# The selective scan of a fused four-layer kernel: VectorE's product of a state with its C rows is issued one recurrence later

## The reference

```python
dt = jax.nn.softplus(ts @ W_dt.T + b_dt)      # b, L, 1024
A = -jnp.exp(A_log)                           # 1024, 16

def step(state, inp):                         # state: b, 1024, 16
    dt_t, B_t, C_t, u_t = inp
    dA = jnp.exp(dt_t[..., None] * A)
    state = state * dA + (dt_t * u_t)[..., None] * B_t[:, None, :]
    y = jnp.einsum('bdn,bn->bd', state, C_t)
    return (state, y)
_, ys = jax.lax.scan(step, init, xs)
y = ys.transpose(1, 0, 2) + x * D
y = y * jax.nn.silu(gate)
return y @ W_out.T
```

## Time and profile before

| | |
|---|---|
| median of 3 runs | 1866.13 us (1865.6 to 1867.11) |
| the profiled execution's own time | 1867.5 us |
| its span, first to last instruction | 1865.7 us |
| TensorE matmuls busy | 1676.6 us, 90% |
| VectorE busy | 1114.2 us, 60% |
| ScalarE busy | 872.7 us, 47% |
| GpSimd busy | 818.6 us, 44% |
| first recurrence of the scan to the end of its last product | 189.3 to 581.3 us |

### The profile page before, as it was taken

One profiled execution on the slowest core, in us unless ns is written; L12 is line 12 of the kernel. 1 busy time (PEld: TensorE's weight loads), 2 busy tenths in 40 slices (PEclk: granted clock), 3 DMA queues, 4 the chain that ended last, 5 costly groups with the idle time before them and its releaser, 6 DMA issues. The chain is left out here.

```text
span 1865.7 us, 24304 instructions
## 1 busy us (share of the span) xinstructions
PE 1676.6 (90%) x8214; PEld 1377.9 (74%) x8214; DVE 1114.2 (60%) x1592; ACT 872.7 (47%) x1761; POOL 818.6 (44%) x416
## 2 busy tenths in 40 slices
PE   5994899999997799897998999999999998799988
PEld 4851787777876688676877787788787877678867
DVE  4326999999997522343725666666666667632232
ACT  2336767676764444232623454444444545433231
POOL 2201888888885464142612222222322224355353
PEclk9997999999999999898998999999999999999989
DMA  3102001010100097001201000100100010134100
GB/s 111 63 1 76 41 21 47 12 56 0 68 0 24 1 364 277 18 1 34 63 25 44 23 23 23 45 22 22 45 22 22 22 57 35 69 135 145 59 18 28
DMA packets 25188, 100.84 MB, mean 54 GB/s; under 512 B 3104, under 2 KB 3360, under 8 KB 22560
## 3 DMA queue, kind: packets, MB, share of 16 engines
q1 hardware_dynamic: 24976, 99.89, 14.9%
q10 hardware_dynamic: 144, 0.07, 0.0%
HBM read 97.72 MB, written 2.23 MB: 54 GB/s over the span
## 5 line engine op out<-in xcount | busy, mean ns | idle before, releaser
L985 PE MATMUL psum<-scratch_s,res_const 128*128 128x256 f32 x1024 | 247.5, 380 | 3.8 <-DVE scratch_s L957 3.8
L1615 POOL TENSOR_TENSOR stretch_turned<-stretch_turned,res_const 128x1024 f32<-128x1024 f32 x32 | 80.3, 2509 | 386.8 <-ACT stretch_turned L1476 386.8
L985 PEld LDWEIGHTS psum<-scratch_s,res_const 128*128 128x128 f32 x1024 | 194.1, 190 | 32.0 <-DVE scratch_s L957 5.8
L858 POOL TENSOR_TENSOR scratch_s<-scratch_s,scan_cm 128x1024 f32<-128x1024 f32 x64 | 150.9, 2358 | 54.2 <-DVE scratch_s L947 54.2
L947 DVE TENSOR_TENSOR_SCAN scratch_s<-psum,scratch_s 128x512 f32<-128x512 f32 x128 | 155.5, 1214 | 4.4 <-ACT psum L899 4.2
L1339 PE MATMUL psum<-opnd_xh,query_wqh 128*128 128x256 f32 x512 | 151.3, 296 | 1.9 <-PEq L94 1.9
L846 POOL TENSOR_TENSOR scratch_s<-scan_bm,scratch_s 128x1024 f32<-128x1024 f32 x64 | 151.0, 2360 | 0.1
L899 ACT ACTIVATE psum<-ssm_dt,ssm_vec 128x255 f32 (+1 forms) x256 | 111.2, 466 | 80.4 <-DVE scratch_s L947 79.9
L1339 PE MATMUL psum<-opnd_xh,query_wql 128*128 128x256 f32 x512 | 145.7, 284 | 0.0
L1339 PE MATMUL psum<-opnd_xl,query_wqh 128*128 128x256 f32 x512 | 145.5, 284 | 0.0
L1484 ACT ACTIVATE stretch_pa<-psum,stretch_nm 128x128 f32<-128x128 f32 x128 | 45.3, 366 | 196.7 <-DVE stretch_nm L1706 196.7
(11 more groups left out here) (269 smaller groups left out, 4322.3 us busy)
## 6 DMA issues: line engine op xcount, KB each, us to landing
mi_dw<-in_dw SPq DMA_DIRECT2D x24, 448.0 KB, 5.5
mi_dm<-in_dm SPq DMA_DIRECT2D x24, 448.0 KB, 6.2
query_raw<-in_w_q SPq DMA_DIRECT2D x8, 1024.0 KB, 4.7
query_raw<-in_w_o SPq DMA_DIRECT2D x8, 1024.0 KB, 4.7
scan_cm<-bc_rows SPq DMA_DIRECT2D x12, 512.0 KB, 4.0
gu_raw<-in_w_gu SPq DMA_DIRECT2D x11, 512.0 KB, 7.3
mlpa_raw<-in_w_mlp SPq DMA_DIRECT2D x7, 768.0 KB, 4.2
mlpa_base<-in_b_mlp SPq DMA_DIRECT2D x7, 768.0 KB, 5.7
```

Source lines behind the costliest of these rows:

```text
L858: nc.gpsimd.tensor_tensor(shared[r][h], shared[r][h], weights(4 * h, 4), ALU.mult).then_inc(weighted_pool, 1)
L985: mm = nc.tensor.matmul(ps_y[r], ident, part[:, n * SEQ:(n + 1) * SEQ], start=False, stop=stop and (n + 1) * SEQ == part.shape[1])
L1615: nc.gpsimd.tensor_tensor(heads(turned[:, :]), heads(turned[:, :]), over_heads(C_SIN, SEQ), ALU.mult).then_inc(q_sine, 1)
```

## The change

In each step of VectorE's program the product of the step before is issued between the shared and the own recurrence, and the product of this step is left to the next. The first step has no product; the last product follows the loops. Each product's waits for TensorE's sums and for the C rows (`weigh_ready`) are issued before the own recurrence of its own step. No operation is added or taken away, and no other engine's program changes.

```diff
+            def recur_shared(s, r, i):
+                if i % 2 == 0:
+                    dve.wait_ge(inflow_pool, s * 2 + i // 2 + 1)
+                dve.wait_ge(decayed, s * 2 * QUADS + 2 * i + 1)
+                nc.vector.tensor_tensor_scan(quarter(r, i), decay_shared[i % 2], quarter(r, i), 0.0,
+                                             ALU.mult, ALU.add).then_inc(scanned, 1)
+
+            def recur_own(s, i):
+                dve.wait_ge(inflow_pe, s * QUADS + i + 1)
+                dve.wait_ge(decayed, s * 2 * QUADS + 2 * i + 2)
+                nc.vector.tensor_tensor_scan(state[i], decay_own[i % 2], state[i], 0.0,
+                                             ALU.mult, ALU.add).then_inc(scanned, 1)
+
+            def weigh_ready(s, i, b):
+                at_least(dve, summed, s * QUADS + i - 3)
+                if i % 2 == 0:
+                    at_least(dve, c_own_in[i // 2], b * 16)
+
+            def weigh(s, i):
+                dve.wait_ge(scanned, s * 2 * QUADS + 2 * i + 2)
+                nc.vector.tensor_tensor(own[i], state[i], weights(NH + 2 * i, 2), ALU.mult).then_inc(weighted, 1)
+
             def body(b, j, switch):
                 for r in range(2):
                     s = b * KI + j * 2 + r
                     for i in range(QUADS):
-                        if i % 2 == 0:
-                            dve.wait_ge(inflow_pool, s * 2 + i // 2 + 1)
-                        dve.wait_ge(decayed, s * 2 * QUADS + 2 * i + 1)
-                        nc.vector.tensor_tensor_scan(quarter(r, i), decay_shared[i % 2], quarter(r, i), 0.0,
-                                                     ALU.mult, ALU.add).then_inc(scanned, 1)
-                        dve.wait_ge(inflow_pe, s * QUADS + i + 1)
-                        dve.wait_ge(decayed, s * 2 * QUADS + 2 * i + 2)
-                        nc.vector.tensor_tensor_scan(state[i], decay_own[i % 2], state[i], 0.0,
-                                                     ALU.mult, ALU.add).then_inc(scanned, 1)
-                        at_least(dve, summed, s * QUADS + i - 3)
-                        if i % 2 == 0:
-                            at_least(dve, c_own_in[i // 2], b * 16)
-                        dve.wait_ge(scanned, s * 2 * QUADS + 2 * i + 2)
-                        nc.vector.tensor_tensor(own[i], state[i], weights(NH + 2 * i, 2), ALU.mult).then_inc(weighted, 1)
+                        recur_shared(s, r, i)
+                        if i > 0:
+                            weigh(s, i - 1)
+                        elif not (isinstance(s, int) and s == 0):
+                            weigh(s - 1, QUADS - 1)
+                        weigh_ready(s, i, b)
+                        recur_own(s, i)
 ...
             pairs(dve, body)
+            weigh(TILES - 1, QUADS - 1)
```

## The result

| | before | changed |
|---|---|---|
| median of runs | 1866.62 us (4 runs, 1865.6 to 1867.84) | 1842.19 us (4 runs, 1840.51 to 1843.6) |
| ratio, 95% interval | | 0.9869 [0.9853, 0.9885] |
| the profiled execution's own time | 1867.5 us | 1840.51 us |
| first recurrence to start of the last product | 391.29 us | 365.76 us |

24.4 us faster, where 20.3 were forecast. The scan alone became 25.5 us shorter: 580.60 - 189.31 before, 552.93 - 187.17 after. The two profiled executions differ by 27.0 us. Behind the scan's last product 0.7 us are lost again.

What follows compares the result with a forecast made beforehand. The prediction took VectorE to bound the scan. It gained 24.9 us inside the steps, gave 4.6 us back at the turns of batches, and so forecast 20.3 us less, 1845.8 us, with a range of 1842 to 1854.

Steps and rivals of the forecast that it cites:

- The bound: In the scan, VectorE sets the pace, with no slack but what lies between its own instructions.
- The wait inside the step: Own recurrence to product on VectorE: 14.1 us of idle time goes and 10.8 us come from earlier starts, together 24.9 us.
- the early start behind a PSUM write: The instruction after an own recurrence starts 0.085 us before that recurrence ends, 10.8 us over 127 places.
- the loop's back edges: Loop turns on VectorE cost 0.13 us behind a product; behind a recurrence up to 1.6 us could be gained, taken as 0.
- Waits that change place: Waits for TensorE's sums and C rows, now before the own recurrence: cost taken as 0, at most 3.8 us.
- ScalarE at the turns: At three turns of batches, VectorE waits for ScalarE's decays after its diagonals: 4.6 us given back.
- What else must keep up: TensorE, GpSimd, ScalarE and SyncE's C rows keep up with a VectorE tile of 11.42 us; TensorE has 0.28 us left.
- TensorE's tile stays under VectorE's: Denies the rival that TensorE takes over with a tile of 11.67 us, 8 us back, 1853.8 us; chance 0.07.
- An early start behind a PSUM write exists: Denies the rival that only the idle time goes, 14.1 us gained, 1855.6 us; chance 0.04.
- Not every instruction waits: Denies the rival that 1.31 us stay between an own recurrence and whatever follows, 1868.5 us; chance 0.07.
- The own recurrence is not held by three waits: Denies the rival that moved waits hold the own recurrence until the product ends, 27.9 us lost, 1871.7 us; chance 0.06.

Runs made afterwards that it cites:

- Run 2: The kernel before, old order, with the waits for TensorE's sums and the C rows moved ahead of the own recurrence: 1857.29 us, ratio 0.995 to the kernel before.
- run 3: The changed kernel with the waits for TensorE's sums and the C rows put back before the product: 1840.48 us, ratio 0.9863 to the kernel before.
- run 6: The changed kernel with ScalarE's decays for the next tile's first step issued before the second set of diagonals: 1836.8 us against 1838.93 for the changed kernel.
- Run 5: One of four inflows of a tile computed twice on TensorE, in the changed kernel: 1855.17 us; in the kernel before: 1865.43 us.
- run 7: The changed kernel with ScalarE's next-tile decays moved earlier, plus TensorE's first shared half summed before its wait for the third product: 1835.46 us.
- run 4: The changed kernel with each product issued behind the own recurrence of the next step: 1848.51 us, ratio 0.9904 to the kernel before.
- run 1: The changed kernel measured again without any edit, as reference: 1838.93 us, ratio 0.9861 to the kernel before.
- run 8: The changed kernel alone and with both moves (ScalarE's decays, TensorE's first shared half) on the same chip: 1841.05 us and 1836.08 us.

## Why the prediction was right, point by point

- **The bound.** VectorE had no slack but between its own instructions. 25.5 us were gained in the scan, all but the 3.4 us of shorter products (below) from there.
- **The number and the range.** The forecast of 1845.8 us was 3.6 too high. 1842.19 lies 0.2 us above the lower end of the range, 1842; the bounds that the prediction worked out ended at 1842.5, and the changed kernel's two later sets (1838.93 and 1841.05 us, on other chips) lie below both. That the number fell inside was luck. The mechanism does not hang on it.
- **The wait inside the step** was put at 24.9 us. The idle time of 14.2 us is gone, and the early start behind a PSUM write is there: 1.13 us from a recurrence of 1.22 us. The value I took, from the pair of attention, was nearly right; the Trainium skill's rule ("VectorE: DVE Perf Modes", section "The DRAIN you can't avoid") would have given nothing, and the trace does not agree with it: 124 of 127 own recurrences are followed by a shared one before they end, the other three wait for ScalarE. The same section adds in its first paragraph that an instruction which is not held starts earlier; with that sentence the trace agrees, and the prediction left it out. Run 2 corrects the reason, though. I wrote that the product waits "because the product reads what the recurrence wrote and waits for its semaphore". Of the 14.2 us only 4.4 are that; 9.8 are met waits, taken up late.
- **Where the size was off.** 5.2 us more were gained in the scan than the 20.3 of the sum. Two terms were mis-sized. I took instruction lengths as fixed, but a product behind an instruction it does not depend on is 0.027 us shorter: 127 x 0.027 = 3.4 us. And the loop's back edges, bounded at 1.6 us and taken at 0, gave 1.4: product to shared recurrence was 0.60 or 0.61 us in 118 of 127 cases and up to 0.88 in the rest, 0.616 in the mean against 0.605, times 127; behind a recurrence the difference vanishes. The other 0.4 are the rest of smaller differences: the early start behind an own recurrence was 0.093 in the mean and not 0.085 (1.220 - 1.127, outside the turns; 1.0 us in all), and some 0.6 go the other way, 0.2 of it at the turns. I should have taken the back edges: they are idle time behind a short instruction that goes under a long one, and rows 4 showed both lengths.
- **Waits that change place** were taken at 0 with an upper bound of 3.8 us; run 3 gives 0.0. Product to own recurrence is 0.58 or 0.59 us in all 127 cases.
- **ScalarE at the turns** was put at 4.6 us. The three starts came 1.5 to 1.7 us late (2.6 and twice 2.79 against 1.13 behind the own recurrence), 4.8 together, and run 6 takes 4.5 of them away by moving ScalarE's work alone.
- **What else must keep up.** TensorE kept up: its wait at the transposes fell from 31.7 to 3.4 us ("some 5" was forecast) and moved in part to the products, where its weight loads now stand 18.3 us instead of 5.2: 13 us more, where "about 0.3 a tile" made some 10. Run 5 shows the margin. GpSimd's wait fell from 0.76 to 0.28 us; I had said half, for a tile of 11.42. The C rows were requested at 280.37, 0.16 us after the late product, and nothing waited for them.
- **Not in the sum: the end of the scan.** TensorE gets the third product of the last tile 1.8 us before the last one (551.09 and 552.93), where it had been 3.05 (577.55 and 580.60), so more of its sums are left when the last product comes. They end 4.3 us after that product's start (551.81 + 5.45 - 552.93), where it had been 3.6; run 7 takes these 0.7 us back.
- **The rivals.** TensorE's tile stays under VectorE's, if barely. An early start behind a PSUM write exists. Not every instruction waits: 124 shared recurrences start before the own one ahead has ended. The own recurrence is not held by three waits. None of the four happened, and for each a run or a row says so.

## What to carry to other kernels

On an engine that bounds a stage, look at the start distances between its own instructions, not at its busy share: here an instruction that reads the output of the one ahead of it, and waits for its semaphore, lost the early start of some 0.09 us and 0.03 us more, and another 0.08 for a wait between the two that had long been met. Put one independent instruction between them; where the order can't change, put the other waits ahead of the producer, which alone gave about a third of this gain. Then work out who has how much left at the new pace before counting the gain: here the stall returned at one place in eight tiles (ScalarE), at the end of the stage (TensorE), and both were bought back by moving a few lines of the late engine's own program.

## What the runs showed of the hardware that I had not expected

- **Met waits are not free behind a running dependence.** One satisfied wait between an own recurrence and the product that needs it costs 0.08 us (1.31 instead of 1.235). A second one, the wait for the C rows, costs 0.03 (1.34) in 40 of its 48 places; in the other 8, the first steps of a pair of tiles in the two middle batches, it costs nothing (1.30 or 1.31), and why is open. Where the product stands behind a recurrence that it does not read, both cost nothing (run 3).
- **An instruction's length depends on what stands ahead of it, and on whether it has waited.** The product takes 692 ns behind the recurrence it depends on (691 in run 2, with one wait), 665 behind the shared recurrence of the next step, and 674 in the mean in run 4. A recurrence behind a product is some 17 ns longer than one behind a recurrence, in either order (own 1221 and 1204, shared 1214 and 1198), so that cancels. It is not only what stands ahead, though: an instruction that starts after the one ahead has ended is the longer one. At the three turns the shared recurrence takes 1.22 us and elsewhere 1.20 in the mean; in run 4 the own recurrence takes 1.23 us in all 27 cases in which it started after the shared one's end, and 1.207 in the mean of the other 101; the one product of the changed kernel that still waits for its own recurrence takes 0.69. The cause was not looked for.
- **TensorE's clock ahead of the scan.** The 2.1 us by which the scan began earlier lie where the granted clock differs between executions of the same code. 1.7 of them arise in one row of matmuls (L675) that starts at 122.00 in the one and 121.97 in the other: ScalarE's first instruction behind it comes at 130.79 and at 129.06. The kernel before, columns as in the earlier trace rows:

```profile
122.00:131.00 9.00, 9.00 (x17) 2.73 (x18) 1.34 (x2) 2.09 (x3) 0.00 (x0) 0.81 0.00 0
```

The same stretch of the changed kernel:

```profile
122.00:131.00 9.00, 9.00 (x21) 2.87 (x22) 1.34 (x2) 3.77 (x5) 0.00 (x0) 1.00 0.00 0
```

TensorE had stood idle for 2.81 us before it in both. In the one the mean granted clock was then 0.81, so part of this stretch ran at the lower level of 1.2 GHz, and 17 matmuls fell into it; in the other it was 1.00, with 21. Over the 50 us from 100 on, the clock was 0.87 before and in run 6, where the scan began at 189.31 and 189.72, and 0.90 and 0.91 in the changed kernel and in run 1, where it began at 187.17 and 187.95. Why one execution keeps the clock there and another does not is open. This is about as large as what run 6 won in its medians, which is why lengths in the scan were read from the traces and the two versions were timed side by side (run 8).
